# Hats of a deformable convolution: their Y planes clipped by an integer output of ScalarE, with a new order of turns and new banks

## The chip, the cores and the metric

The kernel runs on one core of one Trainium2 chip. The metric is the device time of one execution in microseconds; the kernel before has three runs, with a median of 1013.89 us. TensorE (PE in the profile) multiplies matrices into the banks of PSUM, VectorE (DVE), ScalarE (ACT) and GpSimd (POOL) do elementwise work, and SyncE (SP) issues the transfers. Each engine runs its own list of instructions in order; semaphores hold it until another engine is ready.

## The reference, cut to what matters

Sixty-four images of 3 x 84 x 84 go through a stem convolution, a deformable convolution, an attention block whose softmax works on integers, and a feed-forward network (FFN). The change touches the sampling of the deformable convolution:

```python
py = base_y + kh + off[:, :, 0]
px = base_x + kw + off[:, :, 1]
y0, x0 = floor(py), floor(px)
wy, wx = py - y0, px - x0
sampled = v00*(1-wy)*(1-wx) + v01*(1-wy)*wx + v10*wy*(1-wx) + v11*wy*wx   # corners outside count 0
out = einsum('bckhw,ock->bohw', sampled, w) + b
```

Each sampled value is a sum over pixels of the picture times a hat in y times a hat in x, where hat(d) = max(1 - |d|, 0) and d is the distance between a pixel and the sampling place. The kernel computes it in this form, as a matrix product.

## The kernel before, in words

The images are worked in sixteen groups of four (GRP = 4). The work is cut into stages: STEM (stem convolution), HTT (its result transposed, pixels first), OFF and OFS (offsets), HAT and HATW (hats and their products), INT (interpolation as matmuls), DCN (the convolution), LN1X (transposes of the normalised rows), V, FQ (projections), SC (scores), the softmax on VectorE and ScalarE (MAX to PR), PV2 and PV3 (attention output), LN2X, FFN0 to FFN2 (the first FFN product, with the GELU on ScalarE), FF2 (the second) and YO (the store).

What each engine does, and in which order, is written out by hand in the string SLOT: entries such as `pe.FF2.19` mean that TensorE does stage FF2 with a lag of 19 images. One pass through the list is one round, in which every stage handles four images of some group, older groups in the later stages. An image with a lag of 4d + 3 - i is image i (0 to 3) of the group that is d rounds back. In the text, FF2.0 stands for image 0 of a group at stage FF2. Only the order within one engine has an effect; lags of different engines are not compared by the program. BANKS gives the PSUM banks of each stage; a stage of TensorE that takes a bank waits (`free.take`) until the engine that read the bank's last content is done.

Where the diff is: two matmuls of HAT on TensorE (L1179, L1181) write 400 distances in x and 400 in y to two banks, for 126 pixels (six lines of 21) on the partitions, 127 with a shift of one row for odd images. ScalarE's stage HAT (L644, L648) writes their absolute values to HATS: one X plane, and four Y planes, each with another constant subtracted from the distance in y, one for each quarter of the picture. VectorE's stage HAT (L915) turns all five planes, 2000 numbers a row, into min(|d| - 1, 0), which is the hat with its sign changed. VectorE's stage HATW (L921) multiplies the four Y planes by the X plane; the two signs cancel. TensorE's stage INT (L1191, L1193, L1195) multiplies the pixels with these products.

Other lines that the prediction speaks of: L968 casts the queries of a group (stage QKC on VectorE), L1046 and L1003 are scalar_tensor_tensor instructions of the softmax, L1089 is the one of the residual addition, L563 is GpSimd's multiplication of the exponentials by the reciprocal row sums (NRM), which starts when VectorE's reciprocal (RCP, L1059) is done, L686 on ScalarE normalises rows (XH1, XH2), L667 copies transposed rows out of PSUM, L761 is the GELU, and on TensorE L1137 is the stem, L1220 the transposes of LN1X and LN2X, L1246 the second half of a first FFN product, L1258 the query projection, L1327 FF2. L1096 on VectorE adds FF2's result to the residual and so empties FF2's bank.

Of the kernel before, what the change touches and what calls it, by code (L numbers as in the profile page):

```python
# [71 lines left out]
dve.MXB.54 act.XH2.17 pe.INT.9 dve.QQG.55 act.XH2.16 dve.MXC.54 pe.PV3.16 act.V.12 dve.REM.55  # L72
sp.PT.17 dve.DST.54 act.OFF.4 pe.SC.15 pool.RS1.12 dve.EP.55 act.HTT.5 dve.BND.54 pe.STEM1.4
act.LN2X.17 dve.EXP.55 act.SC.13 dve.QQ.54 pe.HTT.6 dve.QQG.54 act.VC.13 dve.EP.54 pe.SC.14 sp.PT.16
act.SQ.14 dve.REM.54 act.DCN.8 pe.INT.8 dve.PREP3.48 dve.SUM.55 act.LN2X.16 pe.LN2X.19 dve.MAX.53
act.VC.12 dve.RCP.55 pool.NRM.17 act.SC.12 pe.V1.12 dve.EXP.54 act.OFS.4 dve.SUM.54 sp.QD.12
pe.LN2X.18 dve.MXB.53 act.LOG.15 dve.MAX.52 act.FFA.16 pe.HTT.5 dve.MXC.53 act.PR.15 dve.PREP0.0
pe.SC.13 dve.MXB.52 act.FFN0.16 dve.DST.53 act.FFN1.16 pe.OFF.4 dve.BND.53 act.FFN2.16 sp.YO0.20
dve.RCP.54 pe.LN2X.17 pool.NRM.16 act.STEM.3 dve.QQ.53 dve.LS1.51 act.LOG.14 pe.DCN.8 dve.LS1.50
act.SQ.13 dve.LS1.49 pe.LN2X.16 act.HAT.7 dve.LS1.48 dve.LN1.48 act.STEM.2 pe.SC.12 dve.VE1.48  # L80
sp.SD.8 act.XH1.11 dve.QQG.53 pe.OFS.4 act.PR.14 dve.REM.53 act.HTT.4 pe.FFA.16 dve.MXC.52 dve.PW.55
pool.RS2A.16 act.XH1.10 pe.FFN0.16 dve.EP.53 act.LN1X.11 dve.DST.52 act.SQ.12 pe.FFN1.16 dve.FF2.59
sp.LX.0 dve.BND.52 act.XH1.9 pe.FFN2.16 dve.PR.55 act.LN1X.10 dve.QQ.52 act.PV2.15 pe.STEM0.0
dve.EXP.53 act.XH1.8 dve.QQG.52 pe.FF2.19 dve.EP.52 act.HAT.6 dve.FF2.58 pe.HAT.7 act.OC.15
pool.RS2.16 sp.LR.12 dve.REM.52 act.LN1X.9 dve.PW.54 pe.FF2.18 dve.SUM.53 act.V.11 dve.HAT.47
pe.HTT.4 act.LOG.13 dve.RCP.53 act.LN1X.8 dve.EXP.52 pe.LN1X.11 act.PR.13 dve.FF2.57 sp.DCN.8
dve.SUM.52 pe.FF2.17 act.LOG.12 dve.RCP.52 act.V.10 dve.PR.54 pe.HAT.6 act.PR.12 pool.NRM.15
dve.FF2.56 dve.HATW.47 pe.LN1X.10 act.FQ0.8 dve.PW.53 act.PV2.14 pe.PV2.15 dve.PR.53 act.FQ1.8
sp.LA.8 dve.PV3.55 pe.LN1X.9 act.OC.14 dve.RES.55 dve.PW.52 act.HAT.5 pe.V0.8 dve.PR.52 act.HAT.4
dve.HAT.46 pe.FF2.16 act.PV2.13 dve.QKC.48 dve.HATW.46 act.INT.7 pool.OFS.4 pe.LN1X.8 dve.HAT.45  # L90
sp.YO1.20 act.VC.11 dve.PV3.54 pe.PV3.15 act.OC.13 dve.HATW.45 act.INT.6 dve.HAT.44 pe.FQ0.8
dve.RES.54 act.PV2.12 dve.LS2.55 pe.PV2.14 act.OC.12 dve.PV3.53 act.HTT.3 dve.LS2.54 pe.FQ1.8
sp.RP.4 dve.RES.53 act.SC.11 dve.HATW.44 pe.HAT.5 act.STEM.1 pool.WDF.0 dve.LN2A.52 act.STEM.0
dve.PV3.52 pe.INT.7 act.HTT.2 dve.PREP1.24 dve.LS2.53 pe.PV2.13 act.VC.10 dve.RES.52 act.INT.5
sp.PT.15 pe.PV3.14 dve.LS2.52 act.SC.10 dve.LN2.52 pe.HAT.4 dve.VE2.52 act.XH2.15 dve.MAX.51
act.INT.4 pe.INT.6 dve.MXB.51 act.XH2.14 dve.MXC.51 pool.NRM.14 pe.HTT.3 act.LN2X.15 dve.DST.51
sp.PT.14 dve.BND.51 act.V.9 pe.PV3.13 dve.MAX.50 act.SQ.11 dve.QQ.51 pe.PV2.12 act.LN2X.14
dve.PREP2.44
# [1311 lines left out]
```

## Time and profile before

| | us |
|---|---|
| runs: median (lowest to highest) | 1013.89 (1013.72 to 1017.25) |
| span of the profiled execution, first to last instruction | 1014.5 |
| TensorE matmuls busy | 880.8 |
| VectorE busy | 876.0 |
| ScalarE busy | 779.8 |
| GpSimd busy | 266.9 |

The profile was taken of a separate execution; its time is known by its span. Busy time counts instructions and not the handling of semaphores. The end of a matmul is modelled, so TensorE's busy time is not time at its peak. The mean granted clock of TensorE over the span is 0.951 of full speed.

### The profile page before, as it was taken

Reading aid. Unit: us, or ns where it says so; the run is one execution under the profiler, and the core shown is the slowest. Engines: PE = TensorE matmul, PEld = TensorE weight load, DVE = VectorE, ACT = ScalarE, POOL = GpSimd, SP = SyncE. Lnnn points to the kernel's source line nnn. Section 1 sums busy time; section 2 is a strip of 40 time slices with the busy share of each in tenths; the row PEclk is TensorE's granted clock in tenths of the full one; section 3 lists DMA queues with packets and bytes.
Section 4 is the critical chain, followed back from the end, with each engine's and each line's share of the span. In section 5 each row is a group of like instructions: output and inputs, shape, how many; then the busy total and the mean of one; then the engine's idle time right before and its main releaser. Section 6 shows DMA issues by size and latency. Waiting matters only on the chain. (4 is left out here: it accounts for less than half of the span.)

```text
span 1014.5 us, 18281 instructions
## 1 busy us (share of the span) xinstructions
PE 880.8 (87%) x5594; PEld 539.9 (53%) x5594; DVE 876.0 (86%) x1695; ACT 779.8 (77%) x1529; POOL 266.9 (26%) x248
## 2 busy tenths in 40 slices
...
## 3 DMA queue, kind: packets, MB, share of 16 engines
...
q14 instruction: 50, 0.40, 0.1%
...
## 5 line engine op out<-in xcount | busy, mean ns | idle before, releaser
L563 POOL TENSOR_TENSOR ee_sb<-ee_sb,rs_sb 128x1020 f32<-128x1020 f32 x64 | 157.2, 2464 | 379.1 <-DVE rs_sb L1059 379.1
L1195 PE MATMUL bank<-hats_sb,ht_sb 127*96 127x400 f32 (+1 forms) x384 | 147.9, 522 | 1.7 <-DVE hats_sb L921 1.7
L1327 PE MATMUL bank<-w_out_sb,ge_sb 128*102 128x192 f32 x768 | 138.8, 331 | 10.9 <-DVE y_sb L1096 6.9
L1327 PEld LDWEIGHTS bank<-w_out_sb,ge_sb 128*102 128x102 f32 x768 | 120.3, 168 | 31.6 <-issue 17.8
L921 DVE TENSOR_TENSOR hats_sb<-hats_sb 126x1600 f32<-126x1600 f32 x64 | 127.2, 1987 | 0.7
L648 ACT ACTIVATE hats_sb<-bank 126x400 f32<-126x400 f32 (+1 forms) x256 | 108.2, 523 | 0.3 <-PE bank L1181 0.3
L727 ACT ACTIVATE a_sb<-scores,sc_sb 128x1020 f16<-128x1020 f32 x64 | 71.1, 1111 | 39.2 <-PE scores L1279 39.2
L1195 PEld LDWEIGHTS bank<-hats_sb,ht_sb 127*96 127x96 f32 (+1 forms) x384 | 58.7, 166 | 72.6 <-issue 69.3
L734 ACT ACTIVATE sq_sb<-rm_sb,sc_sb 128x1020 f32<-128x1020 f16 x64 | 73.5, 1148 | 18.2 <-DVE rm_sb L1031 18.0
L572 POOL TENSOR_TENSOR xshift_sb<-mv_sb,xshift_sb 102x4 f32<-102x4 f32 (+1 forms) x33 | 11.0, 333 | 279.9 <-DVE ve_sb L961 278.5
L1242 PE MATMUL bank<-xt_sb,w_in_sb 128*128 128x408 f32 (+1 forms) x204 | 82.0, 527 | 1.0 <-ACT xt_sb L667 1.0
L915 DVE TENSOR_SCALAR hats_sb<-hats_sb 126x2000 f32<-126x2000 f32 x64 | 76.5, 1195 | 5.9 <-ACT hats_sb L648 5.8
L1046 DVE SCALAR_TENSOR_TENSOR ee_sb<-sq_sb,sc_sb,ep_sb 128x1020 f32<-128x1020 f32 x64 | 79.9, 1249 | 0.1
L1054 DVE TENSOR_REDUCE ss_sb<-ee_sb 128x10 f32<-128x1020 f32 x64 | 77.4, 1209 | 2.1 <-DVE ee_sb L1046 0.5
L1003 DVE SCALAR_TENSOR_TENSOR m_sb<-a_sb,mx_sb 128x1020 f16<-128x1020 f16 x64 | 77.6, 1213 | 0.6
L1220 PE MATMUL bank<-ident_sb,xh_sb 102*128 102x102 f32 x256 | 51.4, 285 | 28.5 <-ACT xh_sb L686 18.3
L740 ACT ACTIVATE ee_sb<-ee_sb 128x1020 f32<-128x1020 f32 x64 | 68.9, 1077 | 9.3 <-POOL ee_sb L563 9.2
L747 ACT ACTIVATE rr_sb<-ee_sb 128x1020 uint16<-128x1020 f32 x64 | 68.6, 1072 | 2.6 <-DVE p_sb L1069 0.7
L1210 PE MATMUL bank<-wdcn_sb,samp_sb 128*100 128x192 f32 x384 | 69.4, 340 | 0.0
L1210 PEld LDWEIGHTS bank<-wdcn_sb,samp_sb 128*100 128x100 f32 x384 | 63.8, 173 | 4.7 <-issue 4.2
L761 ACT ACTIVATE ge_sb<-bank,b_in_sb 128x408 f32<-128x408 f32 (+1 forms) x102 | 51.8, 581 | 12.5 <-PE bank L1246 12.3
L1220 PEld LDWEIGHTS bank<-ident_sb,xh_sb 102*128 102x128 f32 x256 | 28.8, 149 | 58.8 <-ACT xh_sb L686 45.5
(168 smaller groups left out, 1862.7 us busy)
## 6 DMA issues: line engine op xcount, KB each, us to landing
...
q_sb<-qb_sb SPq DMA_DIRECT2D x192, 12.8 KB, 1.9
...
```

The costliest lines, as they stand in the source:

```text
L563: nc.gpsimd.tensor_tensor(EE[b][:], EE[b][:], RS[b][:].unsqueeze(2).to_broadcast([128, RT, TOK]), ALU.mult).then_inc(scaled_done, 1)
L648: nc.scalar.activation(HATS[t.i][0:rows, 1 + j, :], bank[t.banks[1]][0:rows, 0:SMP], ACT.Abs, bias=float(-line)).then_inc(ay_done, 1)
L915: v.tensor_scalar(hat, hat, -1.0, 0.0, ALU.add, ALU.min).then_inc(hat_done, 1)
L921: v.tensor_tensor(hat[:, 1:, :], hat[:, 1:, :], hat[:, 0:1, :].to_broadcast([rows, NCH, SMP]), ALU.mult).then_inc(w_done, 1)
L1003: v.scalar_tensor_tensor(M16[b][:], A16[b][:], MAGIC16 + 128.0, MX[b][:].unsqueeze(2).to_broadcast([128, RT, TOK]), ALU.min, ALU.subtract) ...
L1046: v.scalar_tensor_tensor(EE[b][:].rearrange("p h k -> p (h k)"), SQ[:], sc[:, CC:CC + 1], EP[:].bitcast(bf16), ALU.add, ALU.mult).then_inc ...
L1054: v.tensor_reduce(SS[b][:], EE[b][:], AX.X, ALU.add).then_inc(ss_done, 1)
L1195: last = mm(dst, HT[0:rows, t.i, j, :], HATS[t.i][0:rows, 1 + j, :], start=(j == 0 and not odd), stop=(j == NCH - 2 and odd == 1))
L1210: last = mm(dst, SAMP[:, k, :, :].rearrange("c g p -> c (g p)"), WD[:, k, :], start=False, stop=(k == PACKED - 1))
L1220: last = nc.tensor.transpose(bank[t.banks[0]][:, c * TOK:(c + 1) * TOK], xh[b][:, 64 * c:64 * c + 128], ident[0:TOK, 0:TOK])
L1242: mm(bank[t.banks[first + c]][:, 0:n], weights(k + c, c), src[:, c, :], start=True, stop=False)
L1327: last = mm(bank[t.banks[0]][0:TOK, 0:D], GE[:, f, t.i * TOK:(t.i + 1) * TOK], WOUT[:, f, :], start=(f == 0), stop=(f == FT - 1))
```

## The change

In ScalarE's HAT, the X distances are scaled by 2^-31 before the absolute value. The Y distances are scaled by 2^31 and written through a 32-bit integer view of the same tile. An integer output saturates at 2^31 - 1, so |d| >= 1 ends at this value, which takes the place of the clip. VectorE's HAT clips only the X plane, now min(|d| - 1, 0) x 2^-31, and waits for the X plane alone. VectorE's HATW reads the Y planes as integers, adds -2^31 and multiplies by the X plane in one scalar_tensor_tensor, and waits for the Y planes. Its result is the same product of two hats.

The order in SLOT is new, and so are most banks. The list is cut at another place, which shifts most lags, so it is shown below by engine for the places of TensorE, ScalarE and VectorE that the prediction speaks of.

```diff
+ONE_Y = 2.0 ** 31
...
-BANKS = dict(FFA=(1, 0, 4, 2), STEM0=(5, 4), STEM1=(0, 4), HTT=(5,), OFF=(1,), OFS=(0,), HAT=(5, 0),
-             INT=(3, 2), DCN=(4,), LN1X=(2,), LN2X=(0,), V0=(4, 1), V1=(4, 3), FQ0=(5, 2),
-             FQ1=(0, 4), PV2=(1,), PV3=(4,), FFN0=(5, 3), FFN1=(0, 1), FFN2=(4, 2), FF2=(3,))
+BANKS = dict(FFA=(1, 3, 5, 0), STEM0=(5, 3), STEM1=(1, 4), HTT=(0,), OFF=(1,), OFS=(1,),
+             HAT=(5, 0), INT=(2, 3), DCN=(2,), LN1X=(2,), LN2X=(4,), V0=(1, 3), V1=(1, 5),
+             FQ0=(5, 2), FQ1=(0, 4), PV2=(1,), PV3=(4,), FFN0=(4, 0), FFN1=(2, 5), FFN2=(3, 1),
+             FF2=(4,))
...
-                nc.scalar.activation(HATS[t.i][0:rows, 0, :], bank[t.banks[0]][0:rows, 0:SMP], ACT.Abs).then_inc(ax_done, 1)
+                nc.scalar.activation(HATS[t.i][0:rows, 0, :], bank[t.banks[0]][0:rows, 0:SMP], ACT.Abs,
+                                     scale=1.0 / ONE_Y).then_inc(ax_done, 1)
...
-                    nc.scalar.activation(HATS[t.i][0:rows, 1 + j, :], bank[t.banks[1]][0:rows, 0:SMP], ACT.Abs,
-                                         bias=float(-line)).then_inc(ay_done, 1)
+                    nc.scalar.activation(HATS[t.i][0:rows, 1 + j, :].bitcast(i32), bank[t.banks[1]][0:rows, 0:SMP], ACT.Abs,
+                                         scale=ONE_Y, bias=-line * ONE_Y).then_inc(ay_done, 1)
...
             def hats(t):
-                hat = HATS[t.i][0:t.i % 2 * SHIFT + CH, :, :]
+                hat = HATS[t.i][0:t.i % 2 * SHIFT + CH, 0, :]
                 dve.wait_ge(ax_done, t.count(1, 1))
-                dve.wait_ge(ay_done, t.count(NCH, NCH))
-                v.tensor_scalar(hat, hat, -1.0, 0.0, ALU.add, ALU.min).then_inc(hat_done, 1)
+                v.tensor_scalar(hat, hat, -1.0 / ONE_Y, 0.0, ALU.add, ALU.min).then_inc(hat_done, 1)
 
             def weights(t):
                 rows = t.i % 2 * SHIFT + CH
                 hat = HATS[t.i][0:rows, :, :]
                 dve.wait_ge(hat_done, t.count(1, 1))
-                v.tensor_tensor(hat[:, 1:, :], hat[:, 1:, :], hat[:, 0:1, :].to_broadcast([rows, NCH, SMP]),
-                                ALU.mult).then_inc(w_done, 1)
+                dve.wait_ge(ay_done, t.count(NCH, NCH))
+                v.scalar_tensor_tensor(hat[:, 1:, :], hat[:, 1:, :].bitcast(i32), -ONE_Y,
+                                       hat[:, 0:1, :].to_broadcast([rows, NCH, SMP]), ALU.add, ALU.mult).then_inc(w_done, 1)
```

The order on TensorE from FFN2 to SC.0, the lags left out (a number is the image within its group; V0, FQ0, FQ1 and STEM serve a group or a pair):

```
before: FFN2 STEM0 FF2.0 HAT.0 FF2.1 HTT.3 LN1X.0 FF2.2 HAT.1 LN1X.1 PV2.0 LN1X.2 V0 FF2.3 LN1X.3 PV3.0 FQ0 PV2.1 FQ1 HAT.2 INT.0 PV2.2 PV3.1 HAT.3 INT.1 HTT.0 PV3.2 PV2.3 INT.2 PV3.3 SC.0
after:  FFN2 HAT.0 FF2.0 STEM0 HTT.3 LN1X.0 FF2.1 PV2.0 LN1X.1 HAT.1 FF2.2 LN1X.2 V0 LN1X.3 FF2.3 FQ0 PV2.1 FQ1 HAT.2 INT.0 PV3.0 HAT.3 PV2.2 PV3.1 INT.1 HTT.0 PV3.2 PV2.3 INT.2 PV3.3 SC.0
```

On ScalarE from FFN2 to LN1X.0, and on VectorE from HAT.0 to HATW.3:

```
ScalarE before: FFN2 STEM.0 LOG.1 SQ.2 HAT.0 STEM.1 XH1.0 PR.1 HTT.3 XH1.1 LN1X.0
ScalarE after:  FFN2 HAT.0 XH1.0 SQ.2 STEM.0 LOG.1 HTT.3 LN1X.0
VectorE before: HAT.0 RCP.2 EXP.3 FF2.2 SUM.3 RCP.3 PR.1 FF2.3 HATW.0 PW.2 PR.2 PV3.0 RES.0 PW.3 PR.3 HAT.1 QKC HATW.1 HAT.2 PV3.1 HATW.2 HAT.3 RES.1 LS2.0 PV3.2 LS2.1 RES.2 HATW.3
VectorE after:  HAT.0 PW.1 RCP.2 EXP.3 FF2.2 SUM.3 RCP.3 PR.1 HATW.0 PW.2 PR.2 FF2.3 HAT.1 PW.3 PR.3 QKC HAT.2 HATW.1 PV3.0 HATW.2 RES.0 PV3.1 LS2.0 HAT.3 RES.1 LS2.1 PV3.2 RES.2 LS2.2 HATW.3
```

GpSimd's cycle (RS1 NRM.2 NRM.3 RS2A RS2 NRM.0 OFS NRM.1) stays. On SyncE LX and LR change places, and YO1 goes ahead of LA.

## Rows read from the trace of the kernel before

**Rows 1.** The page, section 1: busy us, share of the span and instructions.
```profile
PE 880.8 (87%) x5594; PEld 539.9 (53%) x5594; DVE 876.0 (86%) x1695; ACT 779.8 (77%) x1529; POOL 266.9 (26%) x248
```

**Rows 2.** Timeline of VectorE: start us, duration us, engine, line, operation, operands.
```profile
202.53 0.58 DVE L968 CAST qb_sb<-qk_sb 128x816 bf16<-128x816 int8 x1
...
870.13 0.58 DVE L968 CAST qb_sb<-qk_sb 128x816 bf16<-128x816 int8 x1
```

**Rows 3.** Busy time by engine in twelve rounds; then PEclk, DMA share, GB/s.
```profile
202.53:870.13 667.60, 629.58 (x4174) 389.34 (x4173) 630.86 (x1213) 576.21 (x1139) 188.31 (x168) 1.00 0.26 55
```

**Rows 4.** Waits of TensorE in the same stretch: us in total, times, longest.
```profile
PE bank L1220 <- ACT xh_sb L686: 9.8, 12, 0.9
PE bank L1258 <- ACT xt_sb L667: 7.7, 12, 0.7
PE bank L1208 <- issue: 4.7, 6, 1.1
PE bank L1220 <- ACT xt_sb L667: 4.3, 12, 0.4
PE scores L1276 <- issue: 3.3, 6, 1.0
```

**Rows 5.** Groups by form, whole span: busy us, mean ns of one, idle before.
```profile
L1046 DVE SCALAR_TENSOR_TENSOR ee_sb<-sq_sb,sc_sb,ep_sb 128x1020 f32<-128x1020 f32 x64 | 79.9, 1249 | 0.1
L1003 DVE SCALAR_TENSOR_TENSOR m_sb<-a_sb,mx_sb 128x1020 f16<-128x1020 f16 x64 | 77.6, 1213 | 0.6
L921 DVE TENSOR_TENSOR hats_sb<-hats_sb 126x1600 f32<-126x1600 f32 x32 | 68.8, 2151 | 0.1
L921 DVE TENSOR_TENSOR hats_sb<-hats_sb 127x1600 f32<-127x1600 f32 x32 | 58.4, 1824 | 0.6
L915 DVE TENSOR_SCALAR hats_sb<-hats_sb 127x2000 f32<-127x2000 f32 x32 | 38.3, 1196 | 4.6 <-ACT hats_sb L648 4.6
L1089 DVE SCALAR_TENSOR_TENSOR x_sb<-pr_sb,sc_in_sb,xr_sb 102x192 f32<-102x192 int8 x64 | 26.2, 410 | 1.6
L879 DVE TENSOR_SCALAR ge_sb<-ge_sb,sc_sb 128x576 f32<-128x576 f32 x1 | 0.5, 521 | 0.0
...
L648 ACT ACTIVATE hats_sb<-bank 126x400 f32<-126x400 f32 x128 | 54.2, 526 | 0.3 <-PE bank L1181 0.3
L715 ACT ACTIVATE qk_sb<-bank 128x408 int8<-128x408 f32 x32 | 14.4, 505 | 5.6 <-PE bank L1264 5.6
```

**Rows 6.** Timeline of VectorE, three products of the hats.
```profile
138.55 3.51 DVE L921 TENSOR_TENSOR hats_sb<-hats_sb 126x1600 f32<-126x1600 f32 x1
...
476.38 2.55 DVE L921 TENSOR_TENSOR hats_sb<-hats_sb 126x1600 f32<-126x1600 f32 x1
...
483.63 1.83 DVE L921 TENSOR_TENSOR hats_sb<-hats_sb 127x1600 f32<-127x1600 f32 x1
```

**Rows 7.** Timeline of GpSimd, two multiplications back to back.
```profile
472.41 4.84 POOL L563 TENSOR_TENSOR ee_sb<-ee_sb,rs_sb 128x1020 f32<-128x1020 f32 x2 [9.48 <-DVE rs_sb L1059]
```

**Rows 8.** Timeline of TensorE from the end of the FFN input.
```profile
459.86 0.96 PE L1246 MATMUL bank<-xt_sb,w_in_sb 64*128 64x408 f32 x4
460.65 1.82 PE L1137 MATMUL bank<-xc_sb,stem_w_sb 49*96 49x441 f32 x4
462.41 2.20 PE L1327 MATMUL bank<-w_out_sb,ge_sb 128*102 128x192 f32 x12
464.53 0.39 PE L1179 MATMUL bank<-rx_sb,lx_sb 9*126 9x400 bf16 x1
464.77 0.34 PE L1181 MATMUL bank<-rx_sb,ly_sb 9*126 9x400 bf16 x1
```

**Rows 9.** Timeline of ScalarE, the last pair of GELUs of that group.
```profile
460.85 1.09 ACT L761 ACTIVATE ge_sb<-bank,b_in_sb 128x408 f32<-128x408 f32 x2 [0.24 <-PE bank L1246]
```

**Rows 10.** Timeline of VectorE in the head: the last hat of group 0.
```profile
49.06 1.20 DVE L915 TENSOR_SCALAR hats_sb<-hats_sb 127x2000 f32<-127x2000 f32 x1 [0.88 <-ACT hats_sb L648]
```

More of the change, by code:

```diff
@@ L71 @@
 |
[L72 to L95, printed above, removed]
@@ L96 @@
[L96 to L98 removed]
+dve.PREP2.44 act.V.15 pe.SC.12 dve.PREP0.-40 act.PR.17 dve.QQG.50 pe.OFS.4 act.LOG.16 dve.EXP.51
+sp.LR.32 dve.REM.50 act.PR.16 pe.FFN0.16 pool.RS1.0 dve.SUM.51 act.FQ0.12 dve.EP.50 pe.FFN1.16
+act.FQ1.12 dve.RCP.51 act.OC.19 dve.EXP.50 pe.FFN2.16 dve.SUM.50 act.HAT.9 dve.MAX.49 pe.HAT.7
+sp.LX.20 act.V.14 dve.RCP.50 act.PV2.18 pe.FF2.19 dve.MXB.49 dve.MXC.49 act.OC.18 pe.STEM0.0
```

26 lines of the change are left out of this document (25 added, 1 removed).

## The prediction

> **What bounds the kernel now.** I read the page first. TensorE and VectorE are busy 87% and 86% of the 1014.5 us span, ScalarE 77%, GpSimd 26% [rows 1]; so shares of the span don't name one engine, and I went to one round. A round is the work on one group of four images. VectorE's cast of the queries (L968) runs once a group, and its first and last issue inside the settled part stand at 202.53 and 870.13 us with twelve rounds between [rows 2]: 667.60 / 12 = 55.63 us a round. Busy times of that stretch [rows 3], divided by 12, give TensorE 52.47, VectorE 52.57 and ScalarE 48.02 us, with the TensorE clock granted in full (1.00). So two engines each leave only about 3.1 us of a 55.6 us round free. ScalarE leaves 7.6.
>
> Which of the two sets the round cannot be told from shares alone, so I asked what TensorE waits for [rows 4]. It is idle 55.63 - 52.47 = 3.16 us a round, and the longest entries are waits on ScalarE: for the normalised rows (9.8 / 12 = 0.82), for the copy of the transposed rows in front of the query projection (7.7 / 12 = 0.64) and between two transposes that share a bank (4.3 / 12 = 0.36). The scores wait 0.28 and the deformable convolution 0.39 for something the view calls issue (their inputs come by DMA). VectorE has no long wait, it is packed. My reading: VectorE's load and TensorE's load are coupled at nearly the same height. Relief of VectorE alone leaves TensorE's 52.47 us and its waits, so a gain needs both the relief and TensorE's waits to shrink.
>
> **The clipping (HAT, L915).** 64 tensor_scalar instructions over 2000 elements a row at 1.196 us [rows 5] become 64 over 400 (the X plane only). No row has this size. Bounds: in proportion, 1.196 x 0.2 = 0.24; above, the same operation over 576 elements takes 0.521. A straight line through both rows (0.473 ns an element) gives 0.44, which I take as it lies between its neighbours. Saved: 0.76 us each, 3.0 a round (bounds 0.67 and 0.96 each, 2.7 to 3.8 a round).
>
> **The product (HATW, L921).** A tensor_tensor over 1600 elements becomes a scalar_tensor_tensor that reads the Y planes as 32-bit integers. The old one costs 1.824 us where nothing disturbs it (127 rows, 32 instructions) [rows 5]. Scalar_tensor_tensor rows: 1020 elements in 1.249 and 1.213 us, 192 in 0.410. A line through 1.249 and 0.410 has 1.013 ns an element and 0.215 us fixed, 1.84 for 1600; in proportion to 1.249 it would be 1.96. No row has a 32-bit integer input; the 192-element row has int8 with f32 and lies where the others do if the part of 0.2 us is fixed. Bounds 1.80 to 1.96; I take 1.84, no change worth counting.
>
> Some products are held up by GpSimd. The one at 476.38 us takes 2.55 instead of 1.83, and GpSimd's multiply by the row sums, under way since before it, ends at 477.25 [rows 6, 7]; one early case takes 3.51. The 126-row form averages 2.151 for that reason; it happens about once a round. In the new order the product of image 0 is moved ahead of the last FFN addition and follows the reciprocal that starts that GpSimd multiply even more closely (one 0.4 us instruction between). So I do not count the 0.7 us as saved: the wait may grow to the 1.68 of the early case. I take +0.9 a round (bounds -0.7 and +1.0).
>
> The Trainium skill, SBUF — State Buffer, section "Who interferes with whom", says that a VectorE instruction with two SBUF inputs contends with a GpSimd instruction that reads SBUF, and whoever starts first holds the shared ports. By that rule the new form is held like the old one, and the trace's 2.55 us at 476.38 agrees for the old form. If the rule did not hold for the new form, VectorE would have 1.6 us a round more room, without a change in the forecast, since TensorE ends last.
>
> VectorE in sum: 52.57 - 3.0 + 0.9 = 50.4 us busy a round. With its present 3.06 us of idle that makes 53.5, so it is no longer last.
>
> **The Y planes on ScalarE (L648).** 256 activations of 0.526 us change scale, bias and output type. ScalarE writes integers elsewhere: int8 over 408 elements in 0.505, f32 over 400 in 0.526 [rows 5], a difference of -0.02. Bounds per instruction -0.02 to +0.02, so at most 0.3 us a round, beside 7.6 us of room. I take 0. If that cover were gone it would cost 0.3 x 15 = 5 us. The X plane only gets a scale: 0. VectorE's HAT now waits for X alone and HATW for the four Y planes; behind the waiting HATW stand softmax instructions of older images, but the Y planes follow the X plane directly on ScalarE (five activations in 2.1 us), and the order keeps other work between HAT and HATW.
>
> **The new order.** The list is cut at another place, so most lags change, but engine by engine it is the same cycle with neighbours exchanged; each stage has the same distance in groups to the one that feeds it. GpSimd's cycle is identical. On SyncE the two residual and patch loads are exchanged, and the store of the second image pair goes ahead of the token load; the addition it waits for is issued on TensorE ahead of the convolution that the token load waits for, so it blocks nothing: 0. The tail after the last product (880 us) has no hats; I count 0 there.
>
> On TensorE three exchanges meet the three long waits on ScalarE. (a) The stem goes from in front of FF2.0 to in front of HTT, and XH1.0 moves ahead of the square and a stem copy on ScalarE, so the 0.82 us wait before LN1X.0 has more in front of it. (b) FF2.2 now lies between LN1X.1 and LN1X.2 (FF2 is 2.2 us of matmuls), which covers the 0.36. (c) FF2.3 lies behind LN1X.3, in front of FQ0, which covers the 0.64. Gone: 1.82 us. The query cast comes earlier by two shortened HATs (1.5 us), which removes the scores' 0.28.
>
> Against that, (d): FF2.0 had the stem's 1.8 us between itself and the end of the FFN input. The last matmul there ends at 460.82 [rows 8], the last pair of GELUs at 461.94 [rows 9], FF2.0 started at 462.41. Now only HAT.0 is between, two matmuls, from 464.53 to 465.11 us here, 0.58 us. The stall: 461.94 - 460.82 - 0.58 = 0.54 us a round. The new banks move drains among stages; every one that I followed has older work in front, but one pair is tight (first rival). I take 0.
>
> **Sum.** TensorE a round: 52.47 + 3.16 - 1.82 - 0.28 + 0.54 = 54.07, against 55.63: 1.56 us less. Fifteen rounds lie between the first and the last group: 23.4 us. In the head the four hats of group 0 run back to back on VectorE, but HAT.3 waited for ScalarE until 49.06 us [rows 10]; only that one's shortened clip and the fixed cost are gained, 0.8 to 1.2 us; I take 1.0. 1014.5 - 24.4 = 990.1. The profiled execution's own time is told by its span only; it stands 0.6 above the median of the runs (1013.89), so I forecast 989.5 us.
>
> **Rivals.** (1) A wait in place of the ones removed, 1001 us, chance 0.17. FF2 gets bank 4, which FQ1 takes next but one. FF2.3's addition now stands behind HATW.0 and two probability instructions on VectorE. If HATW.0 is held for 3.5 us, the addition ends about 1 us after TensorE wants the bank (estimate: 3.5 + 0.9 + 0.4 on VectorE against 2.6 us of FQ0 and an early start of 1 us). Price 0.8 x 15 = 12 us. For it: the held product in [rows 6]. Against it: VectorE now has 2 us of room and runs ahead.
>
> (2) TensorE's waits nearly all go, DCN's and the bank waits too, 0.4 us a round left: 52.9 a round, 2.7 x 15 + 1 = 42 us, 972 us, chance 0.15. For it: with VectorE lighter, ScalarE waits less for it and is early everywhere. Against it: the new GELU wait, and ScalarE's waits for TensorE.
>
> (3) Slower: the integer product at half rate, 0.03. The place is L921. With the part per element doubled it takes 0.215 + 2 x 1.62 = 3.46 us, 1.62 more, four times a round: VectorE 50.4 + 6.5 + 3.06 idle = 60.0 us; (60.0 - 55.63) x 15 = +65, 1079 us. It decides from (55.63 - 53.5) / 4 = 0.5 us more per product, 2.4 us. The 1020-element f16 row at 1.213 us and the int8-f32 row at 0.410 are full rate with no bf16 among the inputs.
>
> The Trainium skill, Vector Engine (DVE) Microarchitecture Reference, section 7 "Points that are easy to get wrong", warns that a scalar_tensor_tensor with two SBUF sources that are not bf16 runs at half throughput. By it the result would be this rival. The trace's f16 row (1.213 us for 1020 elements) speaks against it here.
>
> (4) Slower through ScalarE, 0.04: its room of 7.6 us is used up when a Y activation costs 0.48 more; at twice its cost ScalarE is busy 48.02 + 16 x 0.526 = 56.4 us a round, at least 0.8 x 15 = 12 us more, 1026 us. The int8 row speaks against it. (5) The relief is covered and the exchanges only move waits, within 0.5%: 0.06.
>
> The forecast has 0.55 (its own range 980 to 998). A measurement of this kernel can tell about 0.5%, that is 5 us. Faster: 0.55 + 0.15 + 0.17 less a part of rival 1 that falls short (0.03) = 0.84; same 0.06 + 0.03 = 0.09; slower 0.07. The range goes to rival 2's middle below and past rival 1 above: 970 to 1008.
>
> **What would show it.** HAT's group at 0.40 to 0.48 us; HATW clean at 1.8 to 1.9, one in four longer; VectorE's busy time down by 35 to 50 us in all; ScalarE's Y group unchanged; the L968 casts 54.1 us apart; TensorE waits for ScalarE at L1220 and L1258 gone and a new one of 0.5 us at L1327 on the GELU. Wrong if the casts stay 55 us or more apart with VectorE idle over 5 us a round (then TensorE's waits were never VectorE's or the order's to remove), or if the product is over 2.4 us.

## The result: slower, 1.0079 of the time before

The changed kernel takes 1022.54 us (median of 4 runs), the kernel before beside it 1013.81 (4 runs). The ratio is 1.0079, 95% interval 1.0052 to 1.0106. The forecast was 989.5 us with a range of 970 to 1008: the sign was wrong and the time lies outside the range.

The page after, section 1, to be laid beside [rows 1]:

```profile
PE 876.7 (86%) x5594; PEld 545.0 (53%) x5594; DVE 844.1 (83%) x1695; ACT 782.6 (77%) x1529; POOL 276.0 (27%) x248
```

VectorE has 31.9 us less to do, as wanted. The span grew from 1014.5 to 1019.4 us. The twelve settled rounds between the L972 casts at 200.76 and 872.41 us last 671.65 / 12 = 55.97 us each, against 55.63 in [rows 2] and 54.07 in the forecast: 1.90 x 15 = 28.5 of the 29.3 us by which the forecast's span of 990.1 missed this one. Busy time by engine in single rounds of the changed kernel; the columns are those of [rows 3], behind the length of the stretch:

```profile
200.76:260.74 59.98, 54.78 (x349) 34.88 (x348) 50.33 (x102) 48.33 (x96) 16.00 (x14) 0.94 0.26 51
260.74:318.11 57.37, 52.88 (x349) 33.55 (x348) 50.49 (x101) 48.22 (x96) 15.99 (x14) 0.97 0.26 53
376.16:431.24 55.08, 51.44 (x349) 32.12 (x348) 50.63 (x101) 48.44 (x96) 16.78 (x14) 1.00 0.28 56
597.59:651.44 53.85, 51.25 (x349) 32.08 (x348) 50.62 (x102) 48.20 (x96) 16.79 (x14) 1.00 0.27 58
```

Two kinds of rounds are to be seen. In the seven with the clock granted in full the casts stand 54.73 us apart on average; the same count before (eleven rounds) gives 55.39. So an undisturbed round gained 0.66 us where 1.56 was forecast. In the five others TensorE's clock falls to half, 3.4 us at a time, six times in all; together they are 14.9 us longer than five clean ones. Of these, 9.3 us are TensorE's own busy time (266.4 us in the five, 51.43 in a clean round with all its matmuls on record), the rest is more waiting. Before, the clock fell once. So of the 1.90 us by which a round missed the forecast, 0.66 lie in every round and 14.9 / 12 = 1.24 in the disturbed ones. Waits of TensorE in the twelve rounds (us in total, times, longest), to be laid beside [rows 4]:

```profile
PE bank L1294 <- DMA pt_sb<-p_sb: 17.2, 12, 2.1
PE bank L1212 <- issue: 6.2, 6, 1.4
PE bank L1149 <- ACT hats_sb L652: 5.4, 12, 1.3
PE bank L1304 <- DVE pr_sb L1086: 3.9, 12, 0.3
PE bank L1331 <- ACT ge_sb L765: 3.8, 6, 0.7
PE scores L1280 <- issue: 2.9, 6, 0.7
PE bank L1183 <- DMA rx_sb<-offs_sb: 2.4, 4, 0.8
PE bank L1183 <- ACT ge_sb L765: 1.3, 2, 0.7
PE bank L1224 <- ACT xh_sb L690: 1.0, 1, 1.0
```

The waits of [rows 4] that the exchanges were to remove are gone (9.8 to 1.0; L1258 and the one between two transposes to nothing), and the forecast stall on the GELU is there: (3.8 + 1.3) / 12 = 0.43 us a round, 0.54 forecast. Above them stand waits that the forecast did not have. PV2.0 (L1294) waits 1.43 us a round for the probabilities that a DMA transposes; HTT (L1149) 0.45 for bank 0, which it now shares with HAT; PV3.0 (L1304) 0.33 for VectorE. VectorE has a new wait too, which the kernel before has in no round: its statistics (LS1, ahead of the probabilities PR.0) wait for the DMA that loads the tokens.

```profile
DVE st_sb L950 <- DMA xa_sb<-tok_scratch: 14.8, 11, 2.4
```

Where the clock falls can be read from TensorE's timeline; here around 247 us:

```profile
247.39 0.32 PE L1294 MATMUL bank<-pt_sb,v_sb 102*32 102x102 bf16 x12 [1.89 <-DMA pt_sb<-p_sb]
...
248.47 3.87 PE L1331 MATMUL bank<-w_out_sb,ge_sb 128*102 128x192 f32 x12
```

PV2.0 comes after 1.89 us of idleness; the granted clock is 1.00 up to 248, 0.79 in the microsecond from 248 to 249 and 0.50 in the next two, which is the lower of its two levels; the FF2 behind it takes 3.87 us instead of the 2.2 of [rows 8]. Five of the six low stretches begin within 3 us after a wait of PV2.0 (1.3 to 2.1 us long), the sixth after one of 1.41 us at L1212. Of the eight waits of PV2.0 that are this long, three have no low stretch behind them, among them one of 2.10 us that ends at 419.57.

### The profile page after: what moved, and what is told of

The parts are those of the page before. It is cut to its first block and busy times, and to the rows that moved or that the text cites. A ratio compares the mean times of both kernels' runs of the same rounds, so it can differ in the third digit from the quotient of the medians.

```text
span 1019.4 us, 18281 instructions
## 1 busy us (share of the span) xinstructions
PE 876.7 (86%) x5594; PEld 545.0 (53%) x5594; DVE 844.1 (83%) x1695; ACT 782.6 (77%) x1529; POOL 276.0 (27%) x248
## 5 line engine op out<-in xcount | busy, mean ns | idle before, releaser
L566 POOL TENSOR_TENSOR ee_sb<-ee_sb,rs_sb 128x1020 f32<-128x1020 f32 x64 | 153.8, 2403 | 314.0 <-DVE rs_sb L1063 313.9
L1331 PE MATMUL bank<-w_out_sb,ge_sb 128*102 128x192 f32 x768 | 148.4, 346 | 10.7 <-ACT ge_sb L765 6.8
L925 DVE SCALAR_TENSOR_TENSOR hats_sb<-hats_sb 126x1600 f32<-126x1600 int32 x64 | 139.8, 2187 | 2.3 <-ACT hats_sb L652 2.3
L1331 PEld LDWEIGHTS bank<-w_out_sb,ge_sb 128*102 128x102 f32 x768 | 128.1, 178 | 24.7 <-ACT ge_sb L765 13.5
L652 ACT ACTIVATE hats_sb<-bank 126x400 int32<-126x400 f32 (+1 forms) x256 | 108.4, 525 | 0.3 <-PE bank L1185 0.3
L1050 DVE SCALAR_TENSOR_TENSOR ee_sb<-sq_sb,sc_sb,ep_sb 128x1020 f32<-128x1020 f32 x64 | 82.9, 1295 | 1.4 <-ACT sq_sb L738 0.8
L671 ACT ACTIVATE xt_sb<-bank 128x204 f32<-128x204 f32 x128 | 44.2, 345 | 42.4 <-PE bank L1224 42.4
L1224 PE MATMUL bank<-ident_sb,xh_sb 102*128 102x102 f32 x256 | 51.0, 284 | 12.6 <-ACT xh_sb L690 8.6
L1100 DVE TENSOR_TENSOR y_sb<-bank,x_sb 102x192 f32<-102x192 f32 x64 | 22.5, 352 | 43.4 <-PE bank L1331 43.3
```

Of the source, the lines that this page charges most:

```text
L566: nc.gpsimd.tensor_tensor(EE[b][:], EE[b][:], RS[b][:].unsqueeze(2).to_broadcast([128, RT, TOK]), ALU.mult).then_inc(scaled_done, 1)
L652: nc.scalar.activation(HATS[t.i][0:rows, 1 + j, :].bitcast(i32), bank[t.banks[1]][0:rows, 0:SMP], ACT.Abs, scale=ONE_Y, bias=-line * ONE_Y ...
L925: v.scalar_tensor_tensor(hat[:, 1:, :], hat[:, 1:, :].bitcast(i32), -ONE_Y, hat[:, 0:1, :].to_broadcast([rows, NCH, SMP]), ALU.add, ALU.mu ...
L1050: v.scalar_tensor_tensor(EE[b][:].rearrange("p h k -> p (h k)"), SQ[:], sc[:, CC:CC + 1], EP[:].bitcast(bf16), ALU.add, ALU.mult).then_inc ...
L1331: last = mm(bank[t.banks[0]][0:TOK, 0:D], GE[:, f, t.i * TOK:(t.i + 1) * TOK], WOUT[:, f, :], start=(f == 0), stop=(f == FT - 1))
```

## Experiments

Each kernel ran beside the kernel before. A ratio is its time over that one's, with the 95% interval in brackets; waits are sums over about twelve settled rounds of one profiled execution. Images are numbered within their group; orders are given for the engine named. "Clean" is a round without a low clock.

**The two halves of the change.** First the arithmetic alone, in the old order with the old banks.

```diff
+ONE_Y, scale, i32 view, scalar_tensor_tensor          (as in the change)
 SLOT, BANKS                                           (as before)
```

> The new arithmetic (integer Y planes, clip of the X plane alone, scalar_tensor_tensor) in the order and the banks of before. Theory A, the new order brings the loss: here VectorE gets about 3.3 us a round lighter (4 x 0.84 at HAT), HATW.0 stays held by 0.7 us, TensorE keeps its 3.2 us of waits a round and at most one stretch of lower clock in the settled part, so the time is 1005 to 1012 us, faster than before by up to 0.8%. Rival B, the arithmetic itself brings it (the integer product or the saturating activation disturbs something): slower than before, 1016 to 1024 us. If neither engine's relief counts at all: 1013 us within 2 us.

Ratio 1.0123 [1.0087, 1.0159]. VectorE has 1.8 us less to do in a round, and yet the kernel is slower. The timeline of ScalarE, GpSimd and VectorE shows why:

```profile
418.89 1.17 ACT L737 ACTIVATE sq_sb<-rm_sb,sc_sb 128x1020 f32<-128x1020 f16 x1
420.06 1.89 POOL L565 TENSOR_TENSOR ee_sb<-ee_sb,rs_sb 128x1020 f32<-128x1020 f32 x1 [8.95 <-DVE rs_sb L1062]
420.10 2.93 DVE L1049 SCALAR_TENSOR_TENSOR ee_sb<-sq_sb,sc_sb,ep_sb 128x1020 f32<-128x1020 f32 x1
```

EXP.3 takes 2.93 us, not 1.27. The clip ahead of the reciprocal RCP.2 is 0.84 us shorter, so RCP.2 and the multiply that it releases on GpSimd come earlier. EXP.3 can't come as much earlier: it needs ScalarE's squares, which end at 420.06. So the multiply starts 0.04 us ahead of EXP.3 and holds it; in the kernel before EXP.3 started 0.16 us ahead of the multiply, which began at 472.41 [rows 7]:

```profile
472.25 1.22 DVE L1046 SCALAR_TENSOR_TENSOR ee_sb<-sq_sb,sc_sb,ep_sb 128x1020 f32<-128x1020 f32 x1
```

The addition of image 2 behind EXP.3 is late, and TensorE's FF2.3 waits for it, `L1330 <- DVE y_sb L1099`, 11.4 us in twelve rounds. It is mended by letting EXP.3 start first:

```diff
 VectorE
-HAT.0 RCP.2 EXP.3 FF2.2
+HAT.0 EXP.3 RCP.2 FF2.2
```

> The new arithmetic in the order and banks of before, with one entry of VectorE's order moved: the reciprocal of image 2 (RCP.2) stands behind EXP.3. Where RCP.2 stood in front, the shortened HAT.0 let GpSimd's multiply start 0.1 us ahead of EXP.3, and EXP.3 took 2.93 us instead of 1.27; FF2.2's addition came late and TensorE waited 1.0 us a round for it. Theory E (the flipped start is what ate the relief): EXP.3 is back at 1.3 us in every round, TensorE's wait for y_sb at L1330 falls from 11.4 us in twelve rounds to under 2, the round falls by 1 us, time 1003 to 1009 us. Rival F (the wait moves elsewhere, the order's other waits of TensorE set the round at 55.5 us): over 1015 us.

Ratio 0.999 [0.9959, 1.002], EXP.3 1.28 us, that wait under 0.2. Exchanging two neighbours was worth 1.3% (1.0123 to 0.999; the intervals don't meet). What remains is the effect of the arithmetic in the old order: nothing that the runs can tell. Now the new order and banks with the old arithmetic:

```diff
 HAT, HATW                                             (as before)
+SLOT, BANKS                                           (as in the change)
```

> The new order and banks with the old arithmetic: VectorE clips all five planes (1.2 us) and multiplies with tensor_tensor. Theory A: PV2.0's wait for the transposed probabilities (1.4 us a round in the changed kernel) and the stretches of lower clock stay, and VectorE is 3.3 us a round heavier, so it is slower than the changed kernel: 1030 to 1045 us. Rival B (the arithmetic brings the loss): about the time of before or better, 1000 to 1014 us.

Ratio 1.0567 [1.0514, 1.0619]. The new order with its banks is the loss, and it needs the light arithmetic: with it the same order has 1.0079. Order and banks were not tried apart. TensorE's waits, 203 to 870 us:

```profile
PE bank L1301 <- DVE pr_sb L1083: 27.3, 12, 2.3
PE bank L1291 <- DMA pt_sb<-p_sb: 15.8, 15, 2.2
```

**The new waits.** In the changed kernel PV2.0 goes behind FF2.2, so that the DMA has more time.

```diff
 TensorE
-FF2.1 PV2.0 LN1X.1 HAT.1 FF2.2 LN1X.2
+FF2.1 LN1X.1 HAT.1 FF2.2 PV2.0 LN1X.2
```

> The changed kernel with one entry of TensorE's order moved: PV2.0 stands behind FF2.2 and not behind FF2.1, so its probabilities have 3 us more to arrive. Theory A (TensorE's long wait there costs its 1.4 us a round and is what the clock falls after): the wait at L1294 falls from 17 us in twelve rounds to under 3, up to 0.6 us a round come back as V0's wait for PV2.0's bank, the six stretches of lower clock between 200 and 870 us shrink to two at most, time 1000 to 1010 us. Rival C (the clock falls for another reason, and the wait only moves): 1018 to 1024 us with the stretches still there.

Ratio 1.0153 [1.0111, 1.0194]. The wait of 17.2 is gone and two low stretches are left of six, but a clean round lasts 55.5 us instead of 54.73, V0 waits 5.6 for a bank, and this wait is back:

```profile
PE bank L1224 <- ACT xh_sb L690: 11.6, 13, 1.1
```

The timeline puts it at LN1X.1, which wants XH1.1 and used to stand right behind PV2.0: the wait for the probabilities had covered this one, and the exchange uncovered it. I took it for XH1.3, ahead of which ScalarE's copy of PV2.0 stands, and moved that copy back:

```diff
 ScalarE (on top of the last)
-LN1X.1 PV2.0 STEM.1 XH1.3 LN1X.2
+LN1X.1 STEM.1 XH1.3 PV2.0 LN1X.2
```

> The changed kernel with PV2.0 behind FF2.2 on TensorE, and on ScalarE the rounding of PV2.0 moved behind the last normalised row XH1.3. With the first move alone TensorE's wait for XH1 came back (11.6 us in twelve rounds), because ScalarE stood at PV2.0 in front of XH1.3. Theory A: that wait goes (under 2 us), V0's wait for the bank may grow from 5.6 to 9 us, time 1008 to 1015 us. Rival C (any removed wait comes back elsewhere in the same size): 1020 to 1026 us.

1.0039 [1.0007, 1.007] and one low stretch, but the XH wait stays, 12.7, at LN1X.1 as in the last run. So XH1.1 was moved further forward, on top of that:

```diff
 ScalarE
-SQ.2 STEM.0 LOG.1 HTT.3 LN1X.0 XH1.1
+SQ.2 XH1.1 STEM.0 LOG.1 HTT.3 LN1X.0
```

> The changed kernel with PV2.0 behind FF2.2 on TensorE, and on ScalarE PV2.0 behind XH1.3 and XH1.1 ahead of the stem copy and LOG.1. With the first two moves TensorE still waited 12.7 us in twelve rounds for XH1.1, which stood behind LOG.1, HTT.3 and LN1X.0. Theory T: that wait goes, 0.97 us a round, 1002 to 1008 us. Rival F: 1014 to 1020 us.

1.0044 [1.0019, 1.0068]: the xh wait is gone, and `L1224 <- ACT xt_sb` has 12.7 at the same place: LN1X.1 now waits for the bank that LN1X.0's copy empties. To see whether idleness itself costs, four matmuls of 408 columns, whose result is overwritten, were put ahead of PV2.0's wait in the changed kernel:

```diff
 def pv2(t):
+    if t.i == 0: 4 x mm(bank[t.banks[0]][:, 0:408], WQK[:, 0, 0:128], WIN[:, 0, 0:408])
```

> The changed kernel with four extra matmuls of 408 columns, whose result is overwritten, in front of TensorE's wait for the probabilities of image 0 (PV2.0). They fill some 1.6 us of the 2.1 us that it waits, and change no wait. Theory G (the stretches of lower clock follow that idle time): the six low stretches between 200 and 870 us fall to two at most and the time by 5 to 12 us, 1010 to 1018 us. Rival H (the low stretches have another cause): they stay, 1020 to 1030 us.

1.0218 [1.0173, 1.0263]. PV2.0's wait fell to 0.2 us and the low stretches to three, but the fill lasts 2.9 us of matmuls in each round where 1.43 was to be filled. Whether a fill that fits would pay is left open. The other mishap of the new order, the product HATW.0 that GpSimd holds up, was taken away by letting it start first:

```diff
 VectorE
-HAT.0 PW.1 RCP.2 EXP.3 FF2.2 SUM.3 RCP.3 PR.1 HATW.0
+HAT.0 HATW.0 PW.1 RCP.2 EXP.3 FF2.2 SUM.3 RCP.3 PR.1
```

> The changed kernel with one entry of VectorE's order moved: HATW.0 stands right behind HAT.0, ahead of the reciprocal of image 2, where GpSimd is not multiplying. The hold of 1.7 us at every fourth product goes (mean of L925 from 2.19 to 1.85 us or a little over, since a later GpSimd multiply may meet it). If the hold is on the path (rival D): 1.7 x 15 = 25 us faster, 997 us. If VectorE has room, as theory A says: within 5 us of the changed kernel, 1018 to 1026 us; a few us slower is possible since PV2.0's probabilities don't hang on it but the reciprocals of images 2 and 3 come 1.8 us later.

1.0219 [1.0183, 1.0255]. The hold is gone (126-row form 1.82 us instead of 2.67), but PR.1 behind it comes 1.6 us later in the round. TensorE's waits for transposed probabilities grew from 17.2 to 24.4: PV2.0 still has 16.6 of them, the others are PV2.1's.

**Single exchanges on top of the mended old order (e5).** First the change's exchange (c) with a ScalarE move:

```diff
-TensorE FF2.3 LN1X.3 ; ScalarE STEM.1 XH1.0
+TensorE LN1X.3 FF2.3 ; ScalarE XH1.0 STEM.1
```

> The new arithmetic in the order and banks of before, with RCP.2 behind EXP.3 and with two of the exchanges that the prediction counted on, alone: FF2.3 behind LN1X.3 on TensorE, XH1.0 in front of the stem copy on ScalarE. Theory A (the exchanges work as the prediction says, what failed is what else the new order brought): TensorE's wait in front of the query projection (3.5 to 7.7 us in twelve rounds) goes and that for XH1 falls by half (from 10), 0.8 to 1 us a round, time 990 to 1000 us. Rival F (TensorE's removed waits come back elsewhere): no better than the same kernel without the exchanges, within 3 us.

1.031 [1.0268, 1.0352]; `L1223 <- ACT xt_sb` has 27.7 us, up to 1.9. The transposes wanted their copy earlier and ScalarE's list still had it behind HAT.1. Then XH1.0 alone, far ahead:

```diff
 ScalarE
-HAT.0 STEM.1 XH1.0
+XH1.0 HAT.0 STEM.1
```

> The new arithmetic in the order and banks of before with RCP.2 behind EXP.3, and now one entry of ScalarE's order moved: the first normalised row XH1.0 stands ahead of HAT.0. In the kernel without this move TensorE waits 10.1 us in twelve rounds for XH1.0 and nothing else changes. Theory T (TensorE is what ends last in a round, and a wait that is removed without moving anything on TensorE is gained in full): the wait goes, 0.84 us a round, time 998 to 1003 us. Rival F (the wait comes back elsewhere): within 3 us of the kernel without the move, 1008 to 1014 us.

0.9975 [0.9946, 1.0004], against 0.999 for e5. The first three rows are e5's waits of TensorE in twelve rounds, 197.53 to 861.13 us:

```profile
PE bank L1223 <- ACT xh_sb L689: 10.1, 12, 0.9
PE bank L1261 <- ACT xt_sb L670: 7.9, 12, 0.7
PE bank L1223 <- ACT xt_sb L670: 4.3, 12, 0.4
```

and these are e9's, 203.95 to 866.72 us:

```profile
PE bank L1261 <- ACT xt_sb L670: 7.9, 12, 0.7
PE bank L1330 <- DVE y_sb L1099: 7.3, 12, 0.6
PE bank L1223 <- ACT xt_sb L670: 7.0, 12, 0.6
```

The XH wait of 10.1 is gone, 7.3 came new at FF2.2 and 2.7 at a transpose: 10.0. The shortest rounds last 54.39 us in e5 and 54.34 in e9. Then one more move on ScalarE, for the wait at L1261:

```diff
-LOG.2 LN1X.3
+LN1X.3 LOG.2
```

> As the one before, and on ScalarE the copy of LN1X.3 stands ahead of LOG.2, so that the query projection waits 0.55 us less for it (7.9 us in twelve rounds in the kernel without). Theory T: both waits go, 1.4 us a round, 989 to 996 us. Rival F: 1005 to 1014 us. LOG.2 comes 0.4 us later, which only the probabilities of image 2 see.

1.007 [1.0042, 1.0099]; that wait fell to 3.0, and `L1293 <- ACT v_sb` came with 9.1. The same order (e5's, e9's and this move) with the old arithmetic, to see what the arithmetic is worth in it:

```diff
-ONE_Y, scale, i32 view, scalar_tensor_tensor
+Abs, tensor_scalar over 2000, tensor_tensor          (as before)
```

> The kernel before, with its old arithmetic and banks, and the same three entries moved (RCP.2 behind EXP.3, XH1.0 ahead of HAT.0, LN1X.3 ahead of LOG.2). It tells how much of the gain of the same order with the new arithmetic is the arithmetic. Theory T with VectorE close behind: TensorE can gain 1.4 us a round only as far as VectorE has room (53.8 us a round of instructions and gaps), so 1000 to 1008 us, 6 to 12 us slower than with the new arithmetic. Rival: the arithmetic is worth nothing in any order, and both are alike within 3 us.

1.0109 [1.0067, 1.015]. In this order the arithmetic is worth 0.4% by the ratios (1.0109 to 1.007), and the intervals overlap.

**What sets a clean round.** On top of e5, the same VectorE work at two places: three spare copies of the query plane behind the casts, ahead of a wait of 1.31 us, or ahead of the LN1 statistics, within 34 us in which VectorE waits for nobody. What these and the next expectations call PR.1 is VectorE's scale step of PV3.2 (L1082 before, L1085 in e5), which waits for TensorE's PV3.2; PR.3 is that of PV3.3.

```diff
+for k in range(3): v.tensor_copy(SPARE[k][:], QB[:])
```

> e5 with three spare copies of the 128x816 bf16 Q plane on VectorE, right behind the QKC casts, some 6 us ahead of PR.1's wait of 1.31 us for the projection. The nearest row is the 128x816 cast of 0.59 us, so the three cost 0.9 to 1.7 us a round of VectorE. Theory R (VectorE runs from PR.1 to PW.2, 34 us, without a wait, and work that it has ahead of a wait is only taken from the wait): the wait of L1085 falls by what the copies last, rounds grow by under 0.3 us, 1010 to 1015 us. Rival B (VectorE's busy time counts wherever it lies): +14 to +25 us, 1025 to 1036. Rival T (TensorE's waits set the round): 1011 here and in the next run.

> e5 with the same three copies, but right ahead of the LN1 statistics, in the middle of the stretch of 34 us in which VectorE waits for nobody. Theory R: each round grows by the whole of them, 0.9 to 1.7 us, +13 to +25 us, 1024 to 1036. Rival B: the same as there, but then the run before costs as much. Rival T (TensorE sets the round, VectorE has 4.8 us of slack in 54.4): under +4 us, 1011 to 1015.

0.9976 [0.9942, 1.0009] ahead of the wait, 1.0302 [1.0255, 1.0348] in the run. VectorE's timeline of the first:

```profile
535.51 0.94 DVE L979 COPY spare_sb<-qb_sb 128x816 bf16<-128x816 bf16 x3
...
542.02 0.36 DVE L1089 TENSOR_TENSOR pr_sb<-bank,prow_sb 102x192 int8<-102x192 f32 x1 [0.69 <-PE bank L1307]
```

The wait of 1.31 us became 0.69. The second, GpSimd and VectorE:

```profile
638.14 2.19 POOL L566 TENSOR_TENSOR ee_sb<-ee_sb,rs_sb 128x1020 f32<-128x1020 f32 x1 [2.01 <-DVE rs_sb L1067]
638.49 2.63 DVE L957 COPY spare_sb<-qb_sb 128x816 bf16<-128x816 bf16 x3
```

Here the same copies take 2.63 us, since GpSimd's multiply was under way; rounds grew by 2.1 us, the clock fell eight times in seven of the twelve, and TensorE's wait for y, `L1335 <- DVE y_sb L1104`, rose to 26.9. (I expected at most 1.7 us of copies, and 13 to 25 us for the whole; it is 33.) So VectorE's time added in the run is paid, though most of it here is the hold and not the copies. Is work taken out of it gained? SUM.0 and SUM.1 were left out, a constant in their place, in e5 and in the changed kernel:

```diff
 def exp_sum(t):
-    v.tensor_reduce(SS[b][:], EE[b][:], AX.X, ALU.add)
+    v.memset(SS[b][:], 30000.0) if t.i < 2 else v.tensor_reduce(SS[b][:], EE[b][:], AX.X, ALU.add)
```

> e5 where the sums SUM.0 and SUM.1 of VectorE (1.21 us each, at 22.9 and 25.8 us of the round, inside the stretch without a wait) are left out and a constant stands in their place, so the softmax of these two images is not normalized by its sum. Theory R: 2.0 us a round less up to where the next wait of VectorE begins, so the round loses 1.0 to 2.0 us and the time is 981 to 997. Rival T: TensorE is as busy as before, 1008 to 1013, and VectorE's waits grow by 2.0 us.

> The changed kernel with the same two sums left out (a constant in their place). Theory R, if the new order has the same run of VectorE: 15 to 30 us less than the changed kernel, 992 to 1007. Rival W: in the new order TensorE's waits for the transposing DMA and for bank 0 and the clock's low stretches set the time, and VectorE's own work isn't what they wait for: 1017 to 1023. The wait of PV2.0 for the DMA depends on PR.0, which is VectorE's, so theory R wants it to stay or to move with PR.0.

0.9976 [0.9941, 1.0011] and 1.0019 [0.9987, 1.0051]. Theory R falls: 2.3 us of sums less, and e5's shortest round is 54.43 instead of 54.39. Nearly half went to a second start order that flipped (EXP.1 is held by GpSimd's multiply and takes 2.31 us), the rest into VectorE's waits, 0.74 for ScalarE's squares ahead of EXP.1 and 0.7 for FF2.0. In the changed kernel it gave 0.6% (1.0079 to 1.0019; the intervals just fail to meet) and a shortest round of 53.80 instead of 53.85: the 2.3 us of sums would have been 3% or more. Both at once, e9 with e15:

> e9 (XH1.0 ahead of HAT.0 on ScalarE: TensorE's wait of 0.89 us gone, and FF2.2 waited 0.61 us for VectorE's y.1 in its place) with e15's edit (SUM.0 and SUM.1 left out, the softmax of these two images is not normalized by its sum). Each alone left an undisturbed round at 54.3 to 54.4 us. Theory D (two chains, TensorE's and VectorE's, close at the same point, 41 us after the cast): both together take 0.3 to 0.6 us off a round, 53.8 to 54.1, the y wait of L1330 goes back under 2 us in 12 rounds, and the time is 1000 to 1006 us. Rival T (one engine's total, TensorE's 52 us, or a third chain over ScalarE): 54.3 again, 1009 to 1012 us.

0.9975 [0.9939, 1.0012], shortest round 54.37: theory D falls too. What holds FF2.2 now, TensorE and VectorE of this kernel:

```profile
619.51 2.20 PE L1333 MATMUL bank<-w_out_sb,ge_sb 128*102 128x192 f32 x12
...
621.75 0.36 DVE L1102 TENSOR_TENSOR y_sb<-bank,x_sb 102x192 f32<-102x192 f32 x1 [0.46 <-PE bank L1333]
...
623.20 1.28 DVE L1049 SCALAR_TENSOR_TENSOR ee_sb<-sq_sb,sc_sb,ep_sb 128x1020 f32<-128x1020 f32 x1
...
625.12 0.35 DVE L1102 TENSOR_TENSOR y_sb<-bank,x_sb 102x192 f32<-102x192 f32 x1
...
625.62 0.38 PE L1333 MATMUL bank<-w_out_sb,ge_sb 128*102 128x192 f32 x1 [0.61 <-DVE y_sb L1102]
```

VectorE waits 0.46 us for FF2.0 to end, then has 3.4 us of its list between y.0 and y.1, and FF2.2 cannot start before y.1 has emptied the bank. The wait at FF2.2 is a loop that TensorE itself starts: FF2.0, y.0, 3.4 us of softmax, y.1, FF2.2. Neither e9's nor e15's edit lies in it. The last run keeps all of the work and moves HATW.3 ahead of PV3.2's wait:

```diff
 VectorE (on top of e9)
-HAT.3 RES.1 LS2.0 PV3.2 LS2.1 RES.2 HATW.3 LN2A PV3.3
+HAT.3 HATW.3 RES.1 LS2.0 PV3.2 LS2.1 RES.2 LN2A PV3.3
```

> e9 with VectorE's weights HATW.3 (1.82 us, at 8.4 us of the round, behind PR.1's wait of 1.31 us) moved ahead of that wait, right behind HAT.3. All of the work stays. It fills the wait, PR.1 starts 0.4 us later, and what follows HATW.3 can start up to 1.3 us sooner; MIN.0 needs ScalarE's scores at 11.6, so 0.3 to 0.5 us is left. Theory D: the y wait of FF2.2 goes down by that, the round to 54.0, 1004 to 1009 us. Rival T: 54.3, 1009 to 1012. A third outcome: PR.1 later makes RES.1 and the second LayerNorm no later, since they close on PR.3.

0.9956 [0.9923, 0.9988]: the only version whose interval lies below 1, one of eighteen, and its lead over e9 is within the intervals. The wait was not filled but moved: PV3.2's is gone, and PV3.3 has it, with the cast at 585.27:

```profile
595.54 0.36 DVE L1085 TENSOR_TENSOR pr_sb<-bank,prow_sb 102x192 int8<-102x192 f32 x1 [1.31 <-PE bank L1303]
```

PV3.3's scale step starts 10.3 us behind the cast here as in e5 and e9, and L1085 waits 16.0 us in all against e9's 16.3. So nothing behind it came earlier; the shortest round is 54.39 as in e5, and the y wait stays at 7.5. It is the third outcome of the expectation.

## Why the prediction was wrong

**Right.** The clip takes 355 and 366 ns (0.44 us forecast); the product 1.81 us undisturbed (1.84); ScalarE's Y activations are unchanged. Groups by form in the twelve rounds:

```profile
L925 DVE SCALAR_TENSOR_TENSOR hats_sb<-hats_sb 126x1600 f32<-126x1600 int32 x24 | 64.0, 2666 | 0.0
L925 DVE SCALAR_TENSOR_TENSOR hats_sb<-hats_sb 127x1600 f32<-127x1600 int32 x24 | 43.5, 1813 | 0.0
...
L918 DVE TENSOR_SCALAR hats_sb<-hats_sb 126x400 f32<-126x400 f32 x24 | 8.8, 366 | 0.4
```

VectorE's busy time was 607.06 / 12 = 50.59 us a round (50.4 forecast). The hold of HATW.0 grew from 2.55 to 3.52 us, as feared: it starts 0.11 us behind GpSimd's multiply.

```profile
644.75 1.95 POOL L566 TENSOR_TENSOR ee_sb<-ee_sb,rs_sb 128x1020 f32<-128x1020 f32 x1 [0.16 <-DVE rs_sb L1063]
644.86 3.52 DVE L925 SCALAR_TENSOR_TENSOR hats_sb<-hats_sb 126x1600 f32<-126x1600 int32 x1
```

The Trainium skill, SBUF — State Buffer, section "Who interferes with whom", says that issue order and not the kind of operation decides who blocks. The traces agree: held are this product (+1.7 us), EXP.3 in e1 (+1.7), EXP.1 in e15 (+1.0) and the copies in e14 (+1.7).

**Rival 3** (half rate) is refuted by the 1.813 us. The Trainium skill, Vector Engine (DVE) Microarchitecture Reference, section 7, has the rule behind it; for int32 with f32 this trace disagrees.

**The step that failed first: "the new banks move drains among stages; every one that I followed has older work in front ... I take 0".** I had gone through the waits of the old trace and asked which ones the exchanges end, and did not ask the same of the stages that the exchanges moved forward. PV2.0 went ahead of LN1X.1 and FF2.2 on TensorE while the chain that feeds it went the other way: PR.0 on VectorE starts 39.4 us behind the cast instead of 38.6 (medians of twelve rounds), and the DMA is issued behind it. TensorE used to come to PV2.0 some 6.3 us behind PR.0, now it comes 2.5 us behind. HTT got HAT's bank; PV3.0 meets VectorE late, and HAT its offsets in four rounds. These waits are (17.2 + 5.4 + 3.9 + 2.4) / 12 = 2.4 us a round, more than the 1.82 gained. As prices of single exchanges they are upper bounds, since behind PV2.0's wait lay the one for XH1.1, 11.6 in e3b.

Part of PR.0's delay is a term that the prediction did not have: VectorE's statistics, which stand ahead of PR.0, wait 14.8 us in eleven of twelve rounds for the token load. All eight kernels with the new order have this wait in at least eleven rounds, those with the old order in one at most (e15 and e17). The convolution whose result the load takes comes later behind the cast (ScalarE's copy of it at 26.7 us instead of 25.8, medians). No run took this wait away, so its share of PV2.0's wait is open.

**The second: the sum itself**, "52.47 + 3.16 - 1.82 - 0.28 + 0.54". It takes TensorE's waits as amounts that can be struck out one by one, which left 1.60 us of idle time a round. A clean round has 3.3. e9 struck out 10.1 us and 10.0 came back elsewhere; e3b, e6 and e12 moved the wait from PV2.0 to the normalised rows of image 1 and then to a bank. TensorE's waits are where its list meets loops through the other engines; in these runs ending one made the next longer. What did shrink is the 52.47: TensorE is busy 51.4 us in a clean round. Before, the stem's matmuls lasted 1.82 us [rows 8]: the second half started when the GELU had emptied its bank (461.50, behind the GELU's end at 461.45), and so ran behind the first. Now both run at once, in 0.98 us:

```profile
241.35 0.98 PE L1141 MATMUL bank<-xc_sb,stem_w_sb 49*96 49x441 f32 x4
```

**The third: no term for the clock.** The five disturbed rounds cost 14.9 us, 9.3 of them in slower matmuls, against one such round before; the forecast had the clock at 1.00 throughout. That the low stretches hang on PV2.0's wait is borne out by where they begin and by e3b (six to two), not shown for each. And e3b, with four fewer of them, was no faster: what it gained in the clock it lost in its clean rounds.

**VectorE's relief** I had called needed but not sufficient, and so it is: alone it is worth 0 (e5). The undisturbed timelines show where it went. Before, with the cast at 593.31, HAT.3, RES.1 and the scale step of PV3.2:

```profile
599.45 1.20 DVE L915 TENSOR_SCALAR hats_sb<-hats_sb 127x2000 f32<-127x2000 f32 x1
600.56 0.41 DVE L1089 SCALAR_TENSOR_TENSOR x_sb<-pr_sb,sc_in_sb,xr_sb 102x192 f32<-102x192 int8 x1
...
601.16 0.34 DVE L1082 TENSOR_TENSOR pr_sb<-bank,prow_sb 102x192 int8<-102x192 f32 x1
```

and in e5, with the cast at 584.09:

```profile
589.39 0.36 DVE L917 TENSOR_SCALAR hats_sb<-hats_sb 127x400 f32<-127x400 f32 x1
589.66 0.41 DVE L1092 SCALAR_TENSOR_TENSOR x_sb<-pr_sb,sc_in_sb,xr_sb 102x192 f32<-102x192 int8 x1
...
591.66 0.36 DVE L1085 TENSOR_TENSOR pr_sb<-bank,prow_sb 102x192 int8<-102x192 f32 x1 [1.31 <-PE bank L1303]
```

The residual addition of image 1 comes 1.68 us earlier in the round (7.25 to 5.57), the scale step behind it only 0.28 (7.85 to 7.57): two shortened clips became a wait of 1.31 us for TensorE. The other two lie ahead of the waits for FF2.3 (0.82 us) and for ScalarE's query copies (0.64). In the one profiled execution the shortest round fell by 0.5 us, 54.89 to 54.39, which would be 7.5 us in all; the twelve runs of e5 (1005.69 to 1016.76 us) don't show it, their interval allows 4.

**Left open:** which engine's list would have to change to bring a clean round under 54.3 us in the old order; the loop at FF2.2 is read from the trace, and no run removed VectorE work between y.0 and y.1. Which of the moved waits the new banks cause and which the order, and what the wait for the token load costs, no run tells. Why the head became 1.9 us longer (first cast at 90.99 instead of 89.14) was not tried either.
